# A Mamba layer with a scan of 512 columns per quarter, changed to one scan of four joined quarters with its decays in SBUF

## What is computed

```python
def selective_scan(u, dt, Bm, Cm, A, Dp):

    def step(h, inp):
        u_t, dt_t, B_t, C_t = inp
        dA = jnp.exp(dt_t[..., None] * A)
        h = h * dA + (dt_t * u_t)[..., None] * B_t[:, None, :]
        y = jnp.einsum('bdn,bn->bd', h, C_t)
        return (h, y)
...
x, z = jnp.split(xz, 2, axis=-1)
x = silu(dwconv_causal(x, conv_w, conv_b))
x_dbl = x @ xproj_w.T
dt = jax.nn.softplus(x_dbl[..., :R] @ dt_w.T + dt_b)
...
y = selective_scan(x, dt, Bm, Cm, A, Dp)
return y * silu(z) @ out_w.T
```

## Time and profile before

| what | us |
|---|---|
| median of three executions | 552.32 |
| lowest, highest | 547.97, 553.13 |
| the profiled execution, whole | 551.16 |
| its span, first to last instruction | 549.3 |
| VectorE busy | 483.8 (88%) |
| GpSimd (POOL) busy | 478.5 (87%) |
| TensorE busy | 465.3 (85%) |
| ScalarE busy | 373.3 (68%) |

### The profile page before, as it was taken

The page is one execution under the profiler, slowest core; times in us unless marked ns, Lnnn a source line. Parts: engine busy times, 40 slices in busy tenths (PEclk is TensorE's granted clock), DMA queues, the critical chain, the costliest instruction groups (busy, mean ns, idle before and its releaser), DMA issues.

```text
span 549.3 us, 5677 instructions
## 1 busy us (share of the span) xinstructions
PE 465.3 (85%) x1659; PEld 181.0 (33%) x1659; DVE 483.8 (88%) x602; ACT 373.3 (68%) x656; POOL 478.5 (87%) x153
## 2 busy tenths in 40 slices
PE   6896886979799797979898889888997887795987
PEld 2432322323233232424233424343333332332333
DVE  3679879779898999999999999998899999999951
ACT  2475877476867777786968687858776885374633
POOL 5773889978979989899999999999999999999810
PEclk9897999889979898989999989979899998796999
DMA  5468641765071724426172717181717171700000
GB/s 60 27 48 236 209 155 40 249 217 157 32 242 38 234 78 150 162 93 218 62 231 83 239 63 248 54 253 54 252 50 253 58 253 48 256 16 10 0 11 19
DMA packets 50256, 70.79 MB, mean 129 GB/s; under 512 B 15874, under 2 KB 16818, under 8 KB 50226
## 3 DMA queue, kind: packets, MB, share of 16 engines
q1 hardware_dynamic: 47954, 69.20, 38.5%
q0 software_dynamic: 1024, 1.05, 3.3%
q10 hardware_dynamic: 1248, 0.19, 0.2%
HBM read 58.36 MB, written 9.96 MB: 124 GB/s over the span
## 4 chain that ended last, share of the span: by engine, by line
PE 36%; DVE 32%; issue 15%; ACT 8%; POOL 8%; DMA 0%; DVEq 0%; ACTq 0%; POOLq 0%
DVE st L1600 16%; DVE st L1585 6%; PE ps L638 6%; POOL st L506 5%; PE ps L731 3%; PE ps L719 3%; POOL st L497 2%; ACT ps L1114 2%; PE ps L813 2%; PE ps L549 2%; PE ps L699 2%; PE ps L681 2%; PE ps L829 2%; PE ps L612 2%; PE ps L665 2%
## 5 line engine op out<-in xcount | busy, mean ns | idle before, releaser
L506 POOL TENSOR_TENSOR st<-st,repC 128x2048 f32<-128x2048 f32 x63 | 285.9, 4547 | 21.0 <-ACT carry L1120 13.6
L1600 DVE TENSOR_TENSOR_SCAN st<-ps,carry,st 128x512 f32<-128x512 f32 x192 | 235.2, 1267 | 10.9 <-ACT ps L1114 10.3
L1114 ACT ACTIVATE ps<-dtS,negA 128x512 f32<-128x512 f32 x256 | 170.9, 682 | 47.2 <-DVE st L1600 43.9
L497 POOL TENSOR_TENSOR st<-duS,repB 128x2048 f32<-128x2048 f32 x31 | 141.0, 4548 | 2.0 <-PE ps L719 2.0
L1600 DVE TENSOR_TENSOR_SCAN st<-ps,zero,st 128x512 f32<-128x512 f32 x64 | 78.9, 1269 | 5.8 <-ACT ps L1114 5.4
L719 PE MATMUL ps<-st,fold 128*32 128x512 f32 x504 | 70.4, 625 | 15.4 <-POOL st L506 15.4
L1585 DVE TENSOR_TENSOR st<-duS,ps 128x2048 f32<-128x2048 f32 x32 | 72.7, 2271 | 0.2 <-PE ps L699 0.2
L638 PE MATMUL ps<-act,wT 128*128 128x512 f32 x128 | 57.7, 593 | 0.0
L470 POOL DMA_INDIRECT x<-in_L_tok_ple_table,idx x32 | 31.2, 976 | 12.5 <-issue 9.1
L681 PE MATMUL ps<-xr,wT 128*32 128x512 f32 x32 | 19.6, 697 | 22.5 <-DVE st L1585 22.5
L813 PE MATMUL ps<-xfT,w 97*128 97x512 f32 x64 | 35.2, 642 | 1.3 <-ACT xfT L1139 0.7
(11 more groups left out here) (150 smaller groups left out, 633.1 us busy)
## 6 DMA issues: line engine op xcount, KB each, us to landing
repC<-bc_dram SPq DMA_DIRECT2D x64, 256.0 KB, 4.8
duS<-du_dram SPq DMA_DIRECT2D x60, 256.0 KB, 3.3
dtS<-dt_dram SPq DMA_DIRECT2D x60, 256.0 KB, 4.2
repB<-bc_dram SPq DMA_DIRECT2D x31, 256.0 KB, 3.0
dt_dram<-dt SPq DMA_DIRECT2D x15, 256.0 KB, 3.2
du_dram<-du SPq DMA_DIRECT2D x15, 256.0 KB, 2.0
bc_dram<-bc_sb SPq DMA_DIRECT2D x16, 64.0 KB, 4.7
dtS<-dt SPq DMA_DIRECT2D x4, 256.0 KB, 5.7
```

The lines of the kernel that those rows point to most:

```text
L497: pool.tensor_tensor(st[:, r], duS[:, u % 2], row, ALU.mult).then_inc(sem("dbu_pool"), 1)
L506: pool.tensor_tensor(st[:, r], st[:, r], row, ALU.mult).then_inc(sem("hc_ready"), 1)
L1114: sc.activation(decay_bank(u, r, q), dtS[:, u % 2, q], ACT.Exp, scale=negA[:, way(u), q, r:r + 1]).then_inc(sem("decay_ready"), 1)
L1600: dve.tensor_tensor_scan(st[:, r, q, order], decay_bank(u, r, q)[:, order], st[:, r, q, order], first, ALU.mult, ALU.add).then_inc(sem("sc ...
```

## The change

- A group's four quarters stand in one row of W = 4 x 513 + 1 = 2053 columns: a pad column ahead of each quarter and one at the end (`PADS`). The decay array `dec` is zero in the pads, and `st` holds the carry in them, so that one scan over 2052 columns runs through all four quarters: at a pad the state is multiplied by zero and the carry is added. `keep_last` now writes the pads of `st` in place, and `carry` is gone.
- ScalarE writes the decays to SBUF (`dec`, two groups deep) and no longer to PSUM. A group's four decays stand in a row in its list, and wait once for the scan two groups back.
- The first group of unit 0 and the last group of unit 15 are still scanned in four parts.
- dt times x is made on VectorE from unit 2 on (`du_product`), behind the last scan of a unit, and no longer on GpSimd.
- The three PSUM banks that held decays are used for the rows of B, for the rows of B and C ahead of their copy, and for z. `xr` has three places and no longer four, `zr` two and no longer four, and the rows of C come one by one into six places (before: four at once into eight).
- The order of TensorE's, ScalarE's, VectorE's and SyncE's lists is written anew around four groups a unit, and no longer around 16 scans.

The core of the diff:

```diff
+    W = NQ * (T + 1) + 1
...
-        carry = sb("carry", [P, NR, NQ])
...
-        xr = sb("xr", [P, 4, T])
-        zr = sb("zr", [P, 4, T])
-        st = sb("st", [P, NR, NQ, T])
+        xr = sb("xr", [P, 3, T])
+        zr = sb("zr", [P, 2, T])
+        st = sb("st", [P, NR, W])
+        dec = sb("dec", [P, 2, W])
...
-        repC = sb("repC", [P, 2, NR, T])
+        repC = sb("repC", [P, 6, T])
...
+        def segment(q):
+
+            return slice((T + 1) * q + 1, (T + 1) * q + 1 + T)
+
+        def columns(r):
+            return st[:, r, 1:W].rearrange("p (q t) -> p q t", t=T + 1)[:, :, 0:T]
+
+        PADS = slice(0, W, T + 1)
+
+        def scanned_cols(ap, u):
+            return ap[:, 1:W][:, ::-1] if way(u) else ap[:, 0:W - 1]
...
+            def load_C(u, r):
+                k = NR * u + r
+                wait(sp, "hc_ready", k - 5)
                 sp.wait_ge(sem("bc_in_dram"), 16 * (u + 1))
-                for r in range(NR):
-                    sp.dma_start(repC[:, u % 2, r, :], four_rows(u, 1, r)).then_inc(sem(f"repC_in_{u % 2}"), 16)
+                sp.dma_start(repC[:, k % 6, :], four_rows(u, 1, r)).then_inc(sem(f"repC_in_{k % 6}"), 16)
...
-                pool.tensor_tensor(st[:, r], duS[:, u % 2], row, ALU.mult).then_inc(sem("dbu_pool"), 1)
+                pool.tensor_tensor(columns(r), duS[:, u % 2], row, ALU.mult).then_inc(sem("dbu_pool"), 1)
...
-                row = repC[:, u % 2, r, :].unsqueeze(1).broadcast_to([P, NQ, T])
-                pool.tensor_tensor(st[:, r], st[:, r], row, ALU.mult).then_inc(sem("hc_ready"), 1)
+                row = repC[:, k % 6, :].unsqueeze(1).broadcast_to([P, NQ, T])
+                pool.tensor_tensor(columns(r), columns(r), row, ALU.mult).then_inc(sem("hc_ready"), 1)
...
-                if 0 < u < UNITS - 2:
-                    dt_times_x(u + 2)
...
-                wait(sc, "scanned", scan_nth(u, r, q) - 3)
-                sc.activation(decay_bank(u, r, q), dtS[:, u % 2, q], ACT.Exp,
+                if q == 0:
+                    wait(sc, "scanned", scan_nth(u, r) - 2)
+                sc.activation(dec[:, r % 2, segment(q)], dtS[:, u % 2, q], ACT.Exp,
                               scale=negA[:, way(u), q, r:r + 1]).then_inc(sem("decay_ready"), 1)
...
-                dve.tensor_tensor_scan(st[:, r, q, order], decay_bank(u, r, q)[:, order], st[:, r, q, order],
-                                       first, ALU.mult, ALU.add).then_inc(sem("scanned"), 1)
+            def scan_all(u, r):
+                if r in on_dve(u):
+                    dve.wait_ge(sem("dbu_dve"), dve_nth[u, r])
+                else:
+                    dve.wait_ge(sem("dbu_pool"), pool_nth[u, r])
+                if u:
+                    dve.wait_ge(sem("carried"), scan_nth(u - 1, r))
+                dve.wait_ge(sem("decay_ready"), NQ * scan_nth(u, r))
+
+            def scan(u, r):
+                scan_all(u, r)
+                cols = scanned_cols(st[:, r], u)
+                dve.tensor_tensor_scan(cols, scanned_cols(dec[:, r % 2], u), cols, zero[:, 0:1], ALU.mult, ALU.add) \
+                   .then_inc(sem("scanned"), 1)
...
+            def du_product(u):
+                dve.wait_ge(sem("dt_ready"), u + 1)
+                dve.wait_ge(sem("du_in_dram"), 16 * (u - 1))
+                dve.wait_ge(sem("x_ready"), u + 1)
+                dve.tensor_tensor(du[:], dt[:], x_of(u), ALU.mult).then_inc(sem("du_ready"), 1)
...
```

More of the change, by code:

```diff
@@ L423, in _ @@
             load_B(0)
-            load_C(0)
+            for r in range(NR):
+                load_C(0, r)
             store_bc(1)
@@ L640, in conv, with zed @@
                 mm.then_inc(sem("conv_ps"), 1)
-            def zed(u, bank, at):
-                wait(pe, "z_ready", u)
+            def zed(u):
                 if u == 0:
-                    pe.wait_ge(sem("act_ready"), 4)
+                    pe.wait_ge(sem("bc_in_sbuf"), 2)
                     pe.wait_ge(sem("wT_late"), 1)
[L647 to L652, removed]
+                elif u == 1:
+                    pe.wait_ge(sem("dbu_dve"), dve_nth[0, 0])
+                elif u == 2:
+                    pe.wait_ge(sem("gate_ready"), 2)
+                else:
+                    pe.wait_ge(sem("z_ready"), u)
+                pe.matmul(ps[:, z_bank(u), :], wT[:, 10 + way(u), :], act_at(u, 3), start=True, stop=True) \
                   .then_inc(sem("z_ps"), 1)
@@ L938, in _ @@
[L938 to L947 removed]
+                if quick:
+                    hidden(u - 2, 2)
+                    hidden(u - 2, 3)
@@ L1360, in _ @@
-            for p in range(NR * NQ):
-                decay(0, p // NQ, p % NQ)
-                first_unit(p)
+            sc.wait_ge(sem("rows_ready"), 1)
+            decay(0, 0, 0)
+            softplus_exp(1)
+            decay(0, 0, 1)
+            softplus_plus1(1)
+            softplus_ln(1)
+            decay(0, 0, 2)
+            bc_out(1)
+            decay(0, 0, 3)
+            uT_chunk(2)
+            decays(0, 1)
+            uT_chunk(3, ZED)
+            dt_out(1)
+            keep_last(0, 0)
@@ L1363, in _ @@
+            decays(0, 2)
+            silu_tables()
+            act_silu(2, LONG)
+            act_silu(3, ZED)
+            z_silu(0)
+            z_silu(1)
+            conv_silu(2, PRE)
+            keep_last(0, 1)
+            exp_ln_tables()
+            decays(0, 3)
+            keep_last(0, 2)
+            decays(1, 0)
+            softplus(2)
+            bc_out(2)
             for u in range(1, UNITS):
-                for p in range(NR * NQ):
-                    decay(u, p // NQ, p % NQ)
-                    between(u, p)
+                for r in range(NR):
+                    keep_last(*((u, r - 1) if r else (u - 1, NR - 1)))
+                    decays(*((u, r + 1) if r < NR - 1 else (u + 1, 0)))
+                    between(u, r)
@@ L1761, in _ @@
-            for p in range(NR * NQ):
-                if p < NQ:
-                    first_product(p)
-                scan(0, p // NQ, p % NQ)
-                first_unit(p)
-            for u in range(1, UNITS):
-                for p in range(NR * NQ):
-                    scan(u, p // NQ, p % NQ)
-                    between(u, p)
-            last, before = UNITS - 1, UNITS - 2
-            dve.wait_ge(sem("scanned"), scan_nth(last, NR - 1, NQ - 1))
-            dve.wait_ge(sem(f"repC_in_{last % 2}"), 64 * (last // 2 + 1))
@@ new lines, in _ @@
+            log1p_error(1)
+            first_product(3)
+            first_scan(3)
+            input_product(0, 1)
+            scan(0, 1)
+            start_residual(2)
+            scan(0, 2)
+            input_product(0, 3)
+            start_residual(3)
+            scan(0, 3)
+            last, before = UNITS - 1, UNITS - 2
+            for u in range(1, UNITS):
+                for r in range(NR):
+                    if (u, r) == (last, NR - 1):
+                        scan_all(u, r)
+                        for q in range(NQ):
+                            scan_part(u, r, q, "last_scanned")
+                    else:
+                        scan(u, r)
+                    between(u, r)
```

727 lines of the change are left out of this document (323 added, 404 removed).

## The result

The changed kernel takes 764.99 us (median of four executions, 764.50 to 766.18) against 551.99 before (here the median of four, 547.97 to 553.13). The ratio is 1.388, with a 95% interval of 1.382 to 1.394: 213 us slower. The forecast was 806 us, with 640 to 850 as the range.

What follows compares the result with a forecast made beforehand. GpSimd (95%) and VectorE (94%) were both full, neither alone the bound. Taking turns: 707.8 us steady, some 55 ahead, 29.6 behind, 10 of hand-overs, span 803; forecast 806 us against 552.32, range 640 to 850.

Steps and rivals of the forecast that it cites:

- The term that decides: Steady part: scans with both operands in SBUF and GpSimd's products take turns on one port, 707.8 us for what took 462.7.
- The free case: Rival: the scan doesn't keep GpSimd out; steady part 437.5 us, 527 us against 552; chance 0.15.
- Sharing at half speed: Rival: port shared, not held; each us of scan beside a product costs half a us, 665 us; chance 0.08.
- the shared port: Rival of VectorE and GpSimd sharing their SBUF port at half speed: 665 us; chance 0.08.
- taking turns: Scans and GpSimd's products each cost their own time on the common port: 785 to 850 us; chance 0.74.
- GpSimd's 94 large products: Steady part: 439.7 us busy less 18.2 for dt times x, 421.5 us; strides of 513 columns booked at nothing.
- Hand-overs: Semaphore releases between the engines' turns: eight or so a unit for 15 units, some 0.08 us each, 10 us; bounds 0 and 40.
- The end: The stretch behind the steady part, booked at 29.6 us as in the profile before.
- The scan's length: VectorE's joined scan of 2052 columns: two steps a column and 0.20 us fixed, 4.48 us; taken as 4.5 in the record.
- The place of reading: Scans reading decays from SBUF rather than PSUM: no cheaper by the rows, so nothing booked for it.
- What was said to be hidden: VectorE's other work (8 us a unit), ScalarE (21), TensorE (25), new orders, smaller rings and loads fit within about 45 us a unit.
- Waiting on top of taking turns: Rival: GpSimd runs ahead, VectorE's own products find nothing beside them; some 3 us a unit, 850 us; within the 0.74.

## Why the prediction was right, and where the sum was off

**The term that decides** was right: scans with both operands in SBUF and GpSimd's products take turns, for the whole length of either. It was read from four instructions of 0.81 to 1.31 us; the changed kernel shows it for 62 scans of 4.48 us, and the decays in SBUF alone bring it about. The free case is out: the products did not stay at 4.55. Sharing at half speed is out too: the product at 396.38 ended 4.32 us after the scan did, so it had made next to no headway beside it.

**The number** fell within 640 to 850 only because that range was widened for the shared port. For taking turns itself I gave 785 to 850, and 765 lies 20 us below it: the mechanism came true, and its own range missed.

**The sum was 41 us too high** (806 against 765), and the errors are in its terms. To compare them I laid the products, the scans and dt times x of both engines in one row by their ends, and counted each from the end of the one ahead of it, or from its own start where that came later:

- GpSimd's 94 large products. I booked 421.5 us, and they take 389. I had written that a gain from the stride was excluded since the columns are as many; that step failed. 63 products with C are 0.37 us shorter, 23 us, as the kernel with the stride alone shows. The other 10 us come from products that waited: from the other's end a product with C takes 3.97 us in the median and one with B 4.32, while alone they take 4.15 to 4.18 and 4.5. Products that directly follow another product keep their length.
- The scans. I booked 272.8 us at 4.4 each; 62 times 4.29 are 266, 7 us less, again because all of them waited. Dt times x takes 7.7 and not 8.8 us, 1 us less.
- Hand-overs were booked at 10 us. The time in which none of these instructions is on record is 2.5 us in all from the first product to the last, 7 us less.
- The end was booked as 29.6 us and is 38.7: 9 us the other way. From the first of TensorE's sums for the last group's quarters (L973 at 522.69, now L971 at 729.65) to the end it takes 26.6 us before and 33.1 now. These 6.4 us all lie in the first part, in the rows below. TensorE's granted clock is 0.52 there, near the lower of its two levels (2.4 and 1.2 GHz), and was 1.00; the eight sums take 1062 ns each in the median and not 605. Behind that part both kernels run at 1.00 and agree, 15.63 us and 15.69. The other 2.6 us lie ahead of the sums, where the last scans still take turns, and were not taken apart.

These are 23, 10, 7, 1 and 7 us one way and 9 the other: 39 of the 41 us. The end's first part, before and then now, with the columns of the earlier trace rows:

```profile
522.69:533.61 10.92, 8.56 (x37) 3.85 (x36) 7.11 (x19) 3.73 (x9) 1.09 (x1) 1.00 0.06 14
```

```profile
729.65:747.07 17.42, 15.17 (x37) 6.85 (x37) 5.74 (x17) 3.99 (x9) 0.00 (x0) 0.52 0.04 8
```

The rows for the scan's length from the product's end, VectorE first, then GpSimd:

```profile
417.73 8.45 DVE L1580 TENSOR_TENSOR_SCAN st<-dec,zero,st 128x2052 f32<-128x2052 f32 x1
```

```profile
417.38 4.51 POOL L515 TENSOR_TENSOR st<-duS,repB 128x2048 f32<-128x2048 f32 x1
```

**The scan's length**, 4.48 by two steps a column and 0.20 fixed, is measured as 4.484. The place of reading gave nothing, as booked: with the decays in SBUF the scans of 512 columns that met no product took 1.25 to 1.29 us, against 1.27 from PSUM.

**What was said to be hidden** was hidden: VectorE's products with B stayed at 2.27 us, and moving dt times x back changed the time only by its port time. A unit takes 42.4 us (656.7 for 15.5 units), where I wrote about 45. ScalarE is busy 49% of the span; TensorE is at 70%, not under 60 as I wrote. Its 465.3 us of before would have been 61% of the new span already, and at a lower clock (0.80 in the steady part against 0.93) its matmuls are recorded longer: the sums of states (L719, now L724) went from a mean of 625 ns to 762.

**The free case's price** was too low. I gave 527 us. With 55 scans freed the kernel takes 584, and even its undisturbed units are no shorter than before, as GpSimd waits for ScalarE's pads and TensorE's sums. So the new orders, with the joined scans and without the port, gain nothing that these runs show.

**Waiting on top of taking turns** did not come about with the joined scans (2.5 us with nothing on the port). It did with the scans of 512 columns: 40 us.

## What to carry to other kernels

Ahead of moving a VectorE operand from PSUM to SBUF, look whether GpSimd works beside it: here that one operand made the two engines take turns. It cost 291 us by itself and some 181 of the 213 us of the whole change, against the 31 us that joining the scans was to save. In the profile it doesn't show as idle time but as records that grow, up to 0.3 us short of the sum of two; compare the median length of the same instruction before and after, and count from the end of the other's record. Where two engines are each 95% busy, a short instruction of the rare kind at the edge of the trace (a gather, the last product) can show what a resource does when both want it.

## What was not expected of the hardware

GpSimd's product of 128 x 2048 with an input of four rows of 512 columns took 4.55 us with the rows at a stride of 512, 4.53 at 520, and 4.18 at 513. The stride of the output alone did not matter: with a contiguous large input the median was 4.55 with a contiguous output and 4.57 with one at 513. All the short products had 513 columns in their output too, so whether the input's stride alone is enough was not shown. One column of padding in both arrays made the kernel before a little faster: 545.66 us against 552.36, the median of the kernel before in the same set of executions, ratio 0.983 (0.975 to 0.991).

A VectorE or GpSimd instruction that waits for the other is shorter when counted from the other's end than it is alone, as if its start were already done: 4.29 and 4.48 us for the joined scan, 4.32 and 4.5 for the product with B, 3.97 and 4.16 for the one with C, 0.55 and 0.69 for dt times x.
